# Splitting x by casting and adding DMA transfers, in a conditioned feed-forward kernel

## The reference

```python
xr = x.reshape(Bx, Tx, 8, LATENT)
h = jnp.einsum('btel,elf->btef', xr, W1) + b1
h = jax.nn.gelu(h, approximate=False)
y = jnp.einsum('btef,efl->btel', h, W2) + b2
y = y.reshape(Bx, Tx, Dx)
eo = jax.nn.silu(emb) @ emb_W + emb_b
scale, shift = jnp.split(eo[:, None, :], 2, axis=-1)
hn = _layernorm(y, ln_g, ln_b) * (1.0 + scale) + shift
proj = jax.nn.silu(hn) @ out_W + out_b
return x + proj
```

## Time and profile before

| what | value |
|---|---|
| median of 3 runs | 706.13 us (706.08 to 706.57) |
| span of the profiled execution, from its first to its last instruction | 704.2 us |
| TensorE busy | 700.5 us (99%) |
| VectorE busy | 603.7 us (86%) |
| ScalarE busy | 469.3 us (67%) |
| GpSimd busy | 104.1 us (15%) |
| moved by DMA | 133.22 MB, 189 GB/s in the mean |
| mean granted clock of TensorE | 0.999 |

### The profile page before, as it was taken

How to read it: one execution, slowest core, us unless ns; L and a number is a source line. 1 busy time by engine, 2 the same in 40 slices (tenths; PEclk the granted TensorE clock), 3 DMA queues, 4 the chain that set the end, 5 groups by cost and what they waited for, 6 DMA issues and landing times.

```text
span 704.2 us, 8302 instructions
## 1 busy us (share of the span) xinstructions
PE 700.5 (99%) x3082; PEld 577.9 (82%) x3082; DVE 603.7 (86%) x725; ACT 469.3 (67%) x526; POOL 104.1 (15%) x68
## 2 busy tenths in 40 slices
PE   9999999999999999999999999999999999999998
PEld 6888888888888888888888888888888888888887
DVE  6888999999999989899887999999999978677512
ACT  7898888888878879888883456454656454555500
POOL 0000000000000011100121332423232432322100
PEclk9999999999999999999999999999999999999999
DMA  6766557344232531332789687887699877565531
GB/s 240 247 232 207 187 203 231 109 169 150 90 121 90 209 120 61 120 107 104 210 293 301 183 279 233 275 256 246 219 293 264 256 217 210 183 176 143 156 120 60
DMA packets 51880, 133.22 MB, mean 189 GB/s; under 512 B 4096, under 2 KB 25216, under 8 KB 49408
## 3 DMA queue, kind: packets, MB, share of 16 engines
q1 hardware_dynamic: 46944, 115.79, 46.9%
q0 software_dynamic: 4608, 16.78, 12.3%
q10 hardware_dynamic: 288, 0.13, 0.1%
HBM read 82.35 MB, written 33.55 MB: 165 GB/s over the span
## 4 chain that ended last, share of the span: by engine, by line
PE 99%; DMA 0%; ACT 0%; DVE 0%; issue 0%; DVEq 0%
PE psum L949 48%; PE psum L939 25%; PE psum L923 25%; PE psum L1001 2%; DMA wraw<-in_W 0%; PE psum L971 0%; ACT W L534 0%; DVE res L901 0%; DVEq L125 0%
## 5 line engine op out<-in xcount | busy, mean ns | idle before, releaser
L665 DVE TENSOR_TENSOR g_lo<-g_raw,g_hi 128x1024 fp32r<-128x1024 f32 x128 | 158.4, 1239 | 27.9 <-ACT g_hi L495 25.3
L489 ACT ACTIVATE g_raw<-psum,cols 128x1024 f32<-128x1024 f32 x128 | 142.9, 1116 | 34.1 <-PE psum L923 24.9
L949 PE MATMUL psum<-oW_hi,s_lo 128*128 128x512 f32 x496 | 152.7, 389 | 0.0
L949 PE MATMUL psum<-oW_hi,s_hi 128*128 128x512 f32 x496 | 152.7, 389 | 0.0
L949 PE MATMUL psum<-oW_lo,s_hi 128*128 128x512 f32 x496 | 152.6, 389 | 0.0
L939 PE MATMUL psum<-g_hi,W 128*128 128x512 f32 x512 | 136.8, 389 | 0.0
L923 PE MATMUL psum<-xT_hi,W 128*128 128x512 f32 x508 | 135.8, 389 | 0.0
L939 PEld LDWEIGHTS psum<-g_hi,W 128*128 128x128 f32 x512 | 96.1, 188 | 20.0
L923 PEld LDWEIGHTS psum<-xT_hi,W 128*128 128x128 f32 x508 | 95.3, 188 | 19.8
L949 PEld LDWEIGHTS psum<-oW_hi,s_hi 128*128 128x128 f32 x496 | 93.1, 188 | 19.4
L949 PEld LDWEIGHTS psum<-oW_hi,s_lo 128*128 128x128 f32 x496 | 93.1, 188 | 19.3
(11 more groups left out here) (77 smaller groups left out, 679.8 us busy)
## 6 DMA issues: line engine op xcount, KB each, us to landing
y_scratch<-y_stage SPq DMA_DIRECT2D x32, 512.0 KB, 3.1
yb<-y_scratch SPq DMA_DIRECT2D x16, 1024.0 KB, 4.8
res<-in_x SPq DMA_DIRECT2D x32, 512.0 KB, 6.1
res<-out_b_all POOLq DMA_DIRECT2D x32, 512.0 KB, 4.5
xT_raw<-in_xT SPq DMA_DIRECT2D x31, 512.0 KB, 4.3
out<-res SPq DMA_DIRECT2D x31, 512.0 KB, 4.1
tail_cols<-in_emb_T SPq DMA_DIRECT2D x24, 512.0 KB, 7.2
wraw<-in_out_W SPq DMA_DIRECT2D x16, 256.0 KB, 4.9
```

The source lines that it names most:

```text
L489: nc.scalar.activation(g_raw[:, m % 2], ring(m), ACT.Gelu, bias=cols[:, R_B1 + k:R_B1 + k + 1]).then_inc(gelu_done, 1)
L665: nc.vector.tensor_tensor(g_lo[:, m % 2], g_raw[:, m % 2], g_hi[:, m % 2].bitcast(F32), ALU.subtract).then_inc(glo_done, 1)
L949: mm = nc.tensor.matmul(proj(q)[:, half], v[:, g, cut], w[:, g, half], start=(g == 0 and k == 0), stop=(g == G - 1 and k == 2))
```

## The change

- Item 0 keeps its path and gets a buffer of its own, `x0_raw`.
- Items 1 to 31 have no raw tile. GpSimd issues a DMA from x in DRAM to `xT_hi`, which casts to fp32r (`load_x`). ScalarE writes `xT_lo` = -`xT_hi` (`negate_x`, at the place of `round_x`). GpSimd then issues a second DMA from x to `xT_lo` which adds (`add_x`), so that `xT_lo` = x - `xT_hi`. VectorE's `rest_x` is gone.
- `xT_hi` and `xT_lo` have three slots (`XS`). `load_x(n)` waits until `first` of item n - 3 is done; the very first waits for W2 of group 0.
- GpSimd's queue is now one list: for each n, `load_x(n)`, then `add_x(n - 1)`, with the sums over partitions between them at n = 25, 27 and 28 and after the last.
- SyncE's residual loads for blocks 0 and 1 wait for `s1_done` in place of the low halves; the second comes later by one item.
- TensorE waits for the two landings in place of the two engines' counts.

```diff
+    XS = 3
-        xT_raw = at("xT_raw", [P, 2, TA], R0 + 48 * KB)
-        xT_hi = at("xT_hi", [P, 2, TA], R0 + 56 * KB, F32R)
-        xT_lo = at("xT_lo", [P, 2, TA], R0 + 64 * KB, F32R)
+        xT_hi = at("xT_hi", [P, XS, TA], R0 + 48 * KB, F32R)
+        xT_lo = at("xT_lo", [P, XS, TA], R0 + 60 * KB, F32R)
+        x0_raw = at("x0_raw", [P, TA], R0 + 100 * KB)
...
 @block.sync
-            load_x(1)
             load_raw(1)
             for n in range(N):
-                if n + 2 < N:
-                    sp.wait_ge(xlo_done, n + 1)
-                    load_x(n + 2)
...
                 if n == N - 2:
-                    sp.wait_ge(xlo_done, N)
-                    for q in range(2):
-                        load_res(q)
+                    sp.wait_ge(s1_done, C * (N - 1))
+                    load_res(0)
                 if n == N - 1:
                     sp.wait_ge(s1_done, M)
+                    load_res(1)
                     load_y(2)
...
 @block.gpsimd
-            mean_of(0)
-            mean_of(1)
-            var_of(0)
+            def load_x(n):
+                g, t = ORDER[n]
+                pool.dma_start(xT_hi[:, n % XS], xT[t, g]).then_inc(xhi_landed[n % XS], 16)
+
+            def add_x(n):
+                g, t = ORDER[n]
+                pool.wait_ge(x_negated, n)
+                pool.dma_start(xT_lo[:, n % XS], xT[t, g], accum_op=ALU.add).then_inc(xlo_landed[n % XS], 16)
+
+            pool.wait_ge(w2_landed, 16)
+            load_x(1)
+            load_x(2)
+            add_x(1)
+            for n in range(3, N):
+                pool.wait_ge(s1_done, C * (n - XS + 1))
+                load_x(n)
+                if n == 25:
+                    mean_of(0)
+                if n == 27:
+                    mean_of(1)
+                if n == 28:
+                    var_of(0)
+                add_x(n - 1)
+            add_x(N - 1)
             var_of(1)
...
 @block.scalar
-            def round_x(n):
-                act.wait_ge(x_landed[n % 2], 16 * ((n + n % 2) // 2))
-                nc.scalar.copy(xT_hi[:, n % 2], xT_raw[:, n % 2]).then_inc(xhi_done, 1)
+            def negate_x(n):
+                act.wait_ge(xhi_landed[n % XS], 16 * x_count(n))
+                nc.scalar.activation(xT_lo[:, n % XS], xT_hi[:, n % XS].bitcast(F32), ACT.Identity, scale=-1.0
+                                     ).then_inc(x_negated, 1)
...
 @block.vector
-                if m == 0:
-                    rest_x(1)
-                if c == 3 and n + 2 < N:
-                    rest_x(n + 2)
...
 @block.tensor
-                    if k == 2 and low_part is not None:
-                        pe.wait_ge(xlo_done, low_part)
+                    if k == 2 and low_of is not None:
+                        pe.wait_ge(xlo_landed[low_of % XS], 16 * x_count(low_of))
...
-                        pe.wait_ge(xhi_done, n + 2)
+                        pe.wait_ge(xhi_landed[(n + 1) % XS], 16 * x_count(n + 1))
```

More of the change, by code:

```diff
@@ L224, in cond_ffn_program @@
         mod_step = sem("mod_step")
-        x_landed = [sem(f"x_landed{s}") for s in range(2)]
-        xhi_done = sem("xhi_done")
-        xlo_done = sem("xlo_done")
+        x0_rounded = sem("x0_rounded")
+        x0_rest = sem("x0_rest")
+        xhi_landed = [sem(f"xhi_landed{s}") for s in range(XS)]
+        x_negated = sem("x_negated")
+        xlo_landed = [sem(f"xlo_landed{s}") for s in range(XS)]
         s1_done = sem("s1_done")
@@ L295, in half_of, with x_count @@
             return slice(h * HG, (h + 1) * HG)
+        def x_count(n):
+            return sum(q % XS == n % XS for q in range(1, n + 1))
         oW_rows = out_W.rearrange("(g p) n -> g p n", p=P)
@@ L304, in _ @@
         def _(sp):
-            def load_x(n):
-                g, t = ORDER[n]
-                sp.dma_start(xT_raw[:, n % 2], xT[t, g]).then_inc(x_landed[n % 2], 16)
             def load_raw(j):
@@ L335, in _ @@
                 part = slice(h * BANK, (h + 1) * BANK)
-                sp.dma_start(xT_raw[:, 0, part], xT[0, 0, :, part]).then_inc(x0_landed[h], 16)
+                sp.dma_start(x0_raw[:, part], xT[0, 0, :, part]).then_inc(x0_landed[h], 16)
             sp.dma_start(wraw[:, 0, P:FF], W1[0, :, P:FF]).then_inc(w1_landed, 16)
@@ L535, in _ @@
             act.wait_ge(x0_landed[1], 16)
-            nc.scalar.copy(xT_hi[:, 0, BANK:], xT_raw[:, 0, BANK:]).then_inc(xhi_done, 1)
+            nc.scalar.copy(xT_hi[:, 0, BANK:], x0_raw[:, BANK:]).then_inc(x0_rounded, 1)
             act.wait_ge(w1_landed, 16)
@@ L544, in _ @@
                 if m == 0:
-                    round_x(1)
+                    negate_x(1)
                 if c == 2 and n + 2 < N:
-                    round_x(n + 2)
+                    negate_x(n + 2)
                 if m + 2 < M:
@@ L632, in _ @@
             dve.wait_ge(x0_landed[0], 16)
-            nc.vector.tensor_copy(xT_hi[:, 0, 0:BANK], xT_raw[:, 0, 0:BANK]).then_inc(x0_hi, 1)
+            nc.vector.tensor_copy(xT_hi[:, 0, 0:BANK], x0_raw[:, 0:BANK]).then_inc(x0_hi, 1)
             dve.wait_ge(w0_rounded, 1)
@@ L639, in rest_x0 @@
                 part = slice(h * BANK, (h + 1) * BANK)
-                dve.wait_ge(xhi_done if h else x0_hi, 1)
-                nc.vector.tensor_tensor(xT_lo[:, 0, part], xT_raw[:, 0, part], xT_hi[:, 0, part].bitcast(F32),
-                                        ALU.subtract).then_inc(xlo_done if h else x0_lo, 1)
+                dve.wait_ge(x0_rounded if h else x0_hi, 1)
+                nc.vector.tensor_tensor(xT_lo[:, 0, part], x0_raw[:, part], xT_hi[:, 0, part].bitcast(F32),
+                                        ALU.subtract).then_inc(x0_rest if h else x0_lo, 1)
             rest_x0(0)
@@ L649, in _ @@
             split_raw(0, 1)
[L651 to L654, removed]
             def split_gelu(m):
@@ L905, in _, with first @@
         def _(pe):
-            def first(m, low_part=None):
+            def first(m, low_of=None):
                 n, c = divmod(m, C)
@@ L918, in first @@
                         pe.wait_ge(w_split, 1)
-                    if k == 2 and low_part is not None:
-                        pe.wait_ge(xlo_done, low_part)
+                    if k == 2 and low_of is not None:
+                        pe.wait_ge(xlo_landed[low_of % XS], 16 * x_count(low_of))
                     for h in range(2):
                         half = slice(h * BANK, (h + 1) * BANK)
-                        mm = nc.tensor.matmul(ring(m)[:, half], W[:, g % WS, w, cut], v[:, n % 2, half],
+                        mm = nc.tensor.matmul(ring(m)[:, half], W[:, g % WS, w, cut], v[:, n % XS, half],
                                               start=(k == 0), stop=(k == 2))
@@ L965, in _ @@
                 if k == 0:
-                    pe.wait_ge(xhi_done if h else x0_hi, 1)
+                    pe.wait_ge(x0_rounded if h else x0_hi, 1)
                 if (k, h) == (1, 0):
@@ L969, in _ @@
                 if k == 2:
-                    pe.wait_ge(xlo_done if h else x0_lo, 1)
+                    pe.wait_ge(x0_rest if h else x0_lo, 1)
                 mm = nc.tensor.matmul(ring(0)[:, half], W[:, 0, w, 0:P], v[:, 0, half],
@@ L983, in _ @@
                             pe.wait_ge(w_split, 2 * (LOAD_OF["W", g] + 1))
-                    first(m + 2, n + 2 if c == 2 else None)
+                    first(m + 2, n + 1 if c == 2 else None)
                 if m == M - 1:
```

## The result

The changed kernel takes 714.32 us (median of 4 runs, 713.41 to 714.87), the kernel before 706.33 us in the same comparison: a ratio of 1.0112, with a 95% interval of 1.0097 to 1.0126. It is slower by 8.0 us, where 3.6 us were forecast, and its time lies 4.6 us above the forecast and inside its range. The profiled execution has a span of 712.3 us, 8.1 us more than before.

The account below looks back on a forecast made before the run. TensorE, busy 700.5 of 704.2 us, was taken to bound the kernel, so any wait adds in full. The timed median of 706.1 us plus a 3.6 us stop at the start gave 709.7 us, range 707.2 to 715.0 us.

Parts of the forecast that it names:

- VectorE's relief is worth nothing: All items: the 31 subtractions VectorE loses, 37.8 us, are not on the chain, so worth 0.
- The sign of some 38 us less busy time: What would show the forecast right: VectorE busy some 38 us less in the profile after the change.
- The start is a chain of four links that ends in a stop in chunk 4: Item 1: wait for W2, casting load, negation, adding load landing at 17.5 us; TensorE wants it at 13.86 us.
- Link 1: Item 1: GpSimd waits for `w2_landed`, so the casting load's issue starts at 6.4 us.
- Link 2: Item 1: the casting load takes 5.0 us from issue and lands at 11.4 us.
- Link 3: Item 1: ScalarE's negation, 1.05 us, plus 0.05 us to pass the semaphore, ends at 12.5 us.
- Link 4: Item 1: the adding load takes 5.0 us (bounds 4.4 and 9.7) and lands at 17.5 us.
- The stop, 3.6 us: Middle of chunk 4: TensorE waits from 13.86 to 17.5 us for item 1's low half, added in full.
- The clock falls in the stop: Rival, chance 0.20: TensorE's clock falls to 1.2 GHz at the start's stop, costing 2.7 us more, 712.4 us.
- Later items hidden: Items 2 to 31: the adding load has 9.5 us against a 4.5 us median landing, so cost 0.
- The rival by which nothing shows: Rival, chance 0.10: item 1's two transfers land in 3.2 us each, TensorE never stops, 706.1 us.
- VectorE holding up GpSimd's descriptors: Item 1's two transfers: VectorE's two-port copies could delay each, making the sum up to 1 us too small.

## Why the prediction was wrong

- *TensorE bounds, and any stop is added in full.* Right. The two losses at the start, 5.4 and 2.6 us, make up the 8.1 us to within 0.1 us. (The three shares of the chain that the prediction adds, 48%, 25% and 25%, make 98% and not 97%.)
- *VectorE's relief is worth nothing.* Right: with item 1 moved back, the ratio is 1.0000. The sign of some 38 us less busy time came out at 31 us, because the subtractions had overlapped their neighbours.
- *The start is a chain of four links that ends in a stop in chunk 4.* Right in kind and place. Link 1 came at 6.3 us (6.4 forecast). Link 2 took 3.8 us, not 5.0. Link 3 took 1.06 us, but from the end of the negation to GpSimd's issue it took 0.3 us, not 0.05.
- *Link 4, the adding load, at 5.0 us.* This is the step that failed in the chain: it took 8.0 us. It has two parts. Its floor is 5.1 to 5.2 us with `cond_all` out of the way, where I had taken 4.5 us from the bias add, which reads SBUF. The other 2.9 us are SyncE's 1 MB of `cond_all`, issued from 8.19 us on. I had reasoned from the DMA share of the stretch to a little over the median, and did not ask which transfers stand in SyncE's queue at the moment of the issue. That backlog delays the add before it gets any share, by some 3 us.
- *The stop, 3.6 us.* It was 5.4 us. Link 4 was 3.0 us too short and link 2 1.2 us too long, so that the errors cancel in part, which is luck.
- *The clock falls in the stop.* I held this as a rival at 0.20, with 2.7 us for it, and left it out of the sum. This is the second step that failed, and the larger one: of the 4.6 us above the forecast it is 2.6 us, and the longer stop is 1.8 us. It happened in the profile, the mean clock was below 1.000 in all four executions (0.995 to 0.998), and the price was near, though no row had shown how many matmuls would run slow. With the stop taken at 3.6 us and the one fall in the trace of before at 1.9 us after the last matmul, it should have been the likelier case. 709.7 + 1.8 for the stop + 2.6 for the clock is 714.1 us, against 714.3 measured.
- *Later items hidden.* Right, with 0.2 us of a weight load's wait at item 4 as the only trace of the crowding that was forecast there. The three sums over partitions cost nothing. The upper end of the range, 715.0 us, stood for stops at later items, which did not come; that the time lies inside the range is in this sense luck.
- *The rival by which nothing shows* needed landings of 3.2 us. Item 1's cast, at 3.8 us, came within 0.6 us of that; no cast landed in under 3.3 us and no add in under 5.1 us in any profile. The Trainium skill's formula in "DMA: Bandwidth & Descriptors", section "Anatomy of one DMA", which gave that estimate of 3.2 us, is a little too low for the quickest cast and much too low for the add.
- *VectorE holding up GpSimd's descriptors* (the Trainium skill, "SBUF — State Buffer", section "SBUF: two separate sides"). No run shows it, and none was made to single it out. The first cast was issued beside VectorE's copy and landed in 3.8 us, where the quickest took 3.4 us in the same profile, and with `cond_all` out of the way the add landed in 5.1 us with VectorE's work unchanged.

What stays open: why a fresh transfer on GpSimd's queue gets nothing for some 3 us beside SyncE's backlog and about as many packets as SyncE's after that; whether it is the DRAM source or the cast that makes this add 0.6 to 0.7 us slower than the bias add; and what, beside the clock, spreads the times of one kernel with a stop by 1 to 2 us. None of these was tried.

## What to carry to other kernels

Where, as here, TensorE is busy 99% of the time, moving work from a compute engine to DMA can gain nothing and can lose, and here it lost where there is no earlier work to hide the longer chain, at the launch. Price such a chain transfer by transfer, each with what the other queues have in flight when it is issued, and not by a median. Then ask of every stop of 2.5 us or more, the shortest with a fall in a profile here, whether the clock falls with it or just behind it, and of every wait put into an engine's queue, what stands behind it in that queue.

## What the runs showed of the hardware

- A GpSimd-issued DMA of 512 KB that adds from DRAM landed in 5.1 us at the least over all profiles, and had all 16 engines busy for 3 us of that (0.54 MB at 100.9% in 13 to 16 us). The cast of the same size took 3.3 us at the least, and 9.2 us in the changed kernel where the engines were full.
- A transfer new to GpSimd's queue got 4% of the engines for 3 us beside 94% for SyncE's queue, and then, if the backlog lasted, about half (61% and 44%, with 132 and 136 packets). It was served 4 to 4.5 us after its issue, and 1.6 us after it with SyncE's queue empty. The Trainium skill, "DMA: Bandwidth & Descriptors", section "Queues, rings and completion order", says that each DMA engine takes turns between its queues packet by packet. The later stretch agrees. The first 3 us do not, if the transfer stood ready by then as it did with SyncE's queue empty, which no view shows.
- TensorE's clock fell to 1.2 GHz some 3.8 us after TensorE had stopped (14.1 to 17.9 us) and came back at about 24.7 us, 5.2 us after it had started again. With a stop of 2.5 us it fell in some executions and not in others. In the one that was profiled it fell at about 17.6 us, 1.0 us after TensorE had started again, came back at 21.0 us and cost 1.6 us.
